# Attention front of a four-layer network: 50-row score stacks, and softmax totals spread over their rows through DRAM

## What is computed

```python
h = NUM_HEADS                       # 16, so d_k = 16
q = _proj_heads(in_features, q_proj_weight, h)
k = _proj_heads(in_features, k_proj_weight, h)
v = _proj_heads(in_features, v_proj_weight, h)
scores = jnp.einsum('bhqd,bhkd->bhqk', q, k) / sqrt(d_k) + mask
attn = jax.nn.softmax(scores, axis=-1)
out = jnp.einsum('bhqk,bhkd->bhqd', attn, v)
```

## Time and profile before

| | |
|---|---|
| median of 3 runs | 1889.87 us (1889.86 to 1893.87) |
| profiled execution, its own time | 1896.14 us |
| its span | 1894.4 us |
| granted TensorE clock, mean | 0.931 |
| PE busy | 1632.2 us, 86% |
| ACT busy | 961.6 us, 51% |
| DVE busy | 936.2 us, 49% |
| POOL busy | 489.3 us, 26% |
| SP-issued DMAs | 103.51 MB, 23.4% of 16 engines' span |

### The profile page before, as it was taken

One profiled execution on the slowest core, in us unless ns is written; L12 is line 12 of the kernel. 1 busy time (PEld: TensorE's weight loads), 2 busy tenths in 40 slices (PEclk: granted clock), 3 DMA queues, 4 the chain that ended last, 5 costly groups with the idle time before them and its releaser, 6 DMA issues. The chain is left out here.

```text
span 1894.4 us, 30936 instructions
## 1 busy us (share of the span) xinstructions
PE 1632.2 (86%) x10275; PEld 1117.4 (59%) x10276; DVE 936.2 (49%) x1793; ACT 961.6 (51%) x1531; POOL 489.3 (26%) x516
## 2 busy tenths in 40 slices
PE   5937999999999975999729999999748986898898
PEld 4822223222232224888618888888547986797787
DVE  6723434425425424777653333333275555665785
ACT  3637999999999973344332222222223334333342
POOL 3113112111111111455642222222143103000664
PEclk8968999999999986999959999999968997898999
DMA  4765056246336009321131111111122010000001
GB/s 161 197 183 80 19 79 84 33 66 85 47 50 87 17 15 309 107 83 37 68 117 48 51 52 50 53 50 50 42 95 67 23 37 20 1 1 4 23 23 45
DMA packets 75082, 125.92 MB, mean 66 GB/s; under 512 B 11169, under 2 KB 45601, under 8 KB 71841
## 3 DMA queue, kind: packets, MB, share of 16 engines
q1 hardware_dynamic: 67872, 103.51, 23.4%
q0 software_dynamic: 7104, 21.01, 3.7%
HBM read 74.63 MB, written 49.85 MB: 66 GB/s over the span
## 5 line engine op out<-in xcount | busy, mean ns | idle before, releaser
L685 ACT ACTIVATE probs<-ps_s 128x1024 f32<-128x1024 f32 (+3 forms) x640 | 513.8, 949 | 45.5 <-PE ps_s L731 42.6
L748 PE MATMUL ps_o<-probs,V 128*17 128x512 f32 (+3 forms) x2560 | 297.4, 536 | 8.5 <-POOL probs L673 8.3
L673 POOL TENSOR_SCALAR_AFFINE_SELECT probs<-probs 128x512 f32<-128x512 f32 x128 | 86.4, 677 | 459.6 <-ACT probs L685 455.7
L731 PEld LDWEIGHTS ps_s<-Q_even,K_even 64*128 64x128 f32 x640 | 56.2, 187 | 155.0 <-ACT probs L685 127.6
L731 PE MATMUL ps_s<-Q_even,K_even 64*128 64x512 f32 (+3 forms) x640 | 127.9, 448 | 22.1 <-DMA Q_even<-shift_parts 14.1
L1362 DVE COPY slot_hT<-ps_hT 128x512 f32<-128x512 f32 x72 | 49.8, 692 | 195.1 <-PE ps_hT L1405 195.1
L705 DVE RECIPROCAL inv_denominator<-ps_o 128x512 f32<-128x512 f32 x32 | 107.4, 3358 | 74.4 <-PE ps_o L762 74.4
L698 DVE COPY weighted<-ps_o 128x512 f32<-128x512 f32 x32 | 22.1, 690 | 246.9 <-PE ps_o L748 246.9
L1894 POOL TENSOR_TENSOR h_lo<-h,h_hi 128x512 fp32r<-128x512 f32 x64 | 89.5, 1415 | 185.4 <-DVE h L1940 185.4
L731 PEld LDWEIGHTS ps_s<-Q_odd,K_odd 64*128 64x128 f32 x640 | 55.2, 183 | 139.3 <-ACT probs L685 126.2
L1415 PE MATMUL ps_slot_y<-we_out,slot_hT 128*128 x576 | 136.3, 380 | 0.9 <-DVE slot_hT L1362 0.9
(11 more groups left out here) (282 smaller groups left out, 4007.4 us busy)
## 6 DMA issues: line engine op xcount, KB each, us to landing
slot_rows<-slots_in SPq DMA_DIRECT2D x72, 128.5 KB
qk_parts<-qk_hi SPq DMA_DIRECT2D x8, 1024.0 KB, 4.3
qk_parts<-qk_lo SPq DMA_DIRECT2D x8, 1024.0 KB, 7.2
Q_odd<-qk_parts SPq DMA_DIRECT2D x24, 256.0 KB
K_odd<-qk_parts SPq DMA_DIRECT2D x24, 256.0 KB
Q_even<-qk_parts SPq DMA_DIRECT2D x18, 256.0 KB
K_even<-qk_parts SPq DMA_DIRECT2D x18, 256.0 KB
X<-x SPq DMA_DIRECT2D x8, 512.0 KB, 4.4
```

The lines of the kernel that those rows point to most:

```text
L673: pool.affine_select(out=block_of, in_=block_of, compare_op=ALU.is_ge, fill=0.0, base=0, pattern=[[0, HG], [1, P]], channel_multiplier=-1) ...
L685: act.activation(probs[:, at % PROB_BUFS, 2 * p:2 * p + 2, off:BT], ps_s[:, s % SCORE_BUFS, :, off:BT], ACT.Exp).then_inc(exp_ok, 1)
L731: last = pe.matmul(ps_s[:, s % SCORE_BUFS, h, off:BT], K[j][HALF * h:HALF * h + HALF, p, t * P:(t + 1) * P], Q[j][HALF * h:HALF * h + HALF ...
L748: last = pe.matmul(ps_o[32 * h:32 * h + DH + 1, q % 2, off:BT], k["V"][:, group, SEQ_TILES * b + t, h, :], probs[:, at % PROB_BUFS, h, off ...
```

## The change

The projected q and k are stored in DRAM in the order of the stacks, each slot of a stack on its own: per block 12 DMAs of 256 KB where there were 2 of 1 MB (3 MB for 2 MB). The projection weights are permuted on chip for that (`by_head`). A unit is then loaded by 4 DMAs of 48 rows. A stack has 50 used rows in each half instead of 64, so no row is blanked; the two rows of ones come by DMA from a small table. The softmax totals no longer pass TensorE: SP stores the 17th rows of a slice to a table `totals` in DRAM (4 DMAs), waits until they landed, and loads each broadcast over its head's 16 rows (4 DMAs, `denominator`). `ps_o` is free for TensorE once VectorE has copied it.

```diff
-SHIFT_ROWS, SHIFT_PARTS = 2 * DH, 2
-SLOT_ROWS = (0, DH, 3 * DH)
+STACK_ROWS = 3 * DH
+SHIFT_PARTS = 2
+USED_ROWS = STACK_ROWS + SHIFT_PARTS
...
-STACK_LOADS = 2 * (len(Q_SLOTS) + len(K_SLOTS))
+STACK_LOADS = 4
...
-                    for n, (part, done) in enumerate(((qk_hi, hi_ok), (qk_lo, lo_ok))):
-                        sp.wait_ge(done, 4 * b + 4)
-                        to = io["qk"][n, b * BT // SEQ, :, :, :, t0:t0 + BT].rearrange("m (c g) r t -> (g r) (m c) t", c=DC)
-                        sp.dma_start(to, part[:, j].bitcast(F32)).then_inc(parts_out[j], 16)
+                    for m, slots in enumerate((Q_SLOTS, K_SLOTS)):
+                        to = io["qk"][m, b * BT // SEQ].rearrange("(c g) p s r t -> c r (g p s) t", c=DC)
+                        for wanted, part, done in ((0, qk_hi, hi_ok), (1, qk_lo, lo_ok)):
+                            for c in range(DC):
+                                sp.wait_ge(done, 4 * b + DC * m + c + 1)
+                                for row, slot in enumerate(slots):
+                                    if slot == wanted:
+                                        sp.dma_start(to[c, DH * row:DH * row + DH, :, t0:t0 + BT],
+                                                     part[:, j, DC * m + c].bitcast(F32)).then_inc(parts_out[j], 16)
...
-                pool.wait_ge(zero_ok, 1)
-                pool.wait_ge(w_lo_ok, 3)
-                blank_rows(pool, k["first_stacks"][0], k["first_stacks"][1], 1.0, blank_ok)
+                pool.memset(ones[:, :], 1.0).then_inc(ones_ok, 1)
...
 def load_stacks(eng, io, g, b, Q, K, sem):
 
-    for slots, dst, m in ((Q_SLOTS, Q, 0), (K_SLOTS, K, 1)):
-        for row, part in zip(SLOT_ROWS, slots):
-            for side in range(2):
-                src = io["qk"][part, b, m, bass.ds(g, 1)].rearrange("o (p s d) t -> s d (o p) t", s=2, d=DH)[side]
-                at = HALF * side + row
-                eng.dma_start(dst[at:at + DH].bitcast(F32), src).then_inc(sem, 16)
+    for m, stack in enumerate((Q, K)):
+        for side in range(2):
+            src = io["qk"][m, b, bass.ds(g, 1)].rearrange("o p s r t -> s r (o p) t")[side]
+            at = HALF * side
+            eng.dma_start(stack[at:at + STACK_ROWS].bitcast(F32), src).then_inc(sem, 16)
...
                     for q in range(SLICES):
+                        sp.wait_ge(sums_ok, SLICES * u + q + 2)
+                        for h in range(HG):
+                            sp.dma_start(io["totals"][q % 2, h:h + 1, :], sums[32 * h + DH:32 * h + DH + 1, q % 2]
+                                         ).then_inc(totals_out, 16)
+                        sp.wait_ge(totals_out, 16 * HG * (SLICES * u + q + 1))
+                        for h in range(HG):
+                            sp.dma_start(denominator[32 * h:32 * h + DH, q % 2],
+                                         io["totals"][q % 2, h:h + 1, :].to_broadcast([DH, BT])
+                                         ).then_inc(spread[q % 2], 16)
                         sp.wait_ge(result_ok, SLICES * u + q + 1)
...
             def _(pool):
-                blank_rows(pool, Q[1], K[1], 1.0, blank_ok)
...
                         dve.wait_ge(pv_ok, NT * u + LAST[q] + 1)
+                        if n >= 2:
+                            dve.wait_ge(spread[q % 2], 16 * HG * (n // 2))
                         dve.tensor_copy(sums[:, q % 2], ps_o[:, q % 2]).then_inc(sums_ok, 1)
...
-                        dve.wait_ge(picked_ok, n + 1)
-                        dve.reciprocal(inv[:, :], ps_o[:, q % 2]).then_inc(norm_ok, 1)
+                        dve.wait_ge(spread[q % 2], 16 * HG * (n // 2 + 1))
+                        dve.reciprocal(inv[:, :], denominator[:, q % 2]).then_inc(norm_ok, 1)
...
                     if t == 0 and n >= 2:
-                        pe.wait_ge(norm_ok, 3 * (n - 2) + 1)
+                        pe.wait_ge(sums_ok, n)
...
-                    pe.matmul(ps_o[:, q % 2], rows, sums_hi[:, :], start=True, stop=False)
-                    pe.matmul(ps_o[:, q % 2], rows, sums_lo[:, :], start=False, stop=True).then_inc(picked_ok, 1)
```

More of the change, by code:

```diff
@@ L174, in _ @@
                                base=0, pattern=[[-1, P]], channel_multiplier=1).then_inc(picked, 1)
[L176 to L180, removed]
+        @block.vector
+        def _(dve):
+            dve.wait_ge(picked, 2)
+            dve.tensor_reduce(k["head_sum"][:, :], k["ident"][:, :].rearrange("p (d h) -> p h d", d=DH), AX.X, ALU.add
+                              ).then_inc(picked, 1)
+            dve.wait_ge(picked, 3)
+            dve.tensor_copy(k["head_sel"][:, :], k["head_sum"][:, :]).then_inc(picked, 1)
 def layer_norm(k, mem, stem):
@@ L262, in phase_qkv, with raw_by_head, by_head @@
         x_view = io["x"].rearrange("(n p) d -> p n d", p=P)
+        def raw_by_head(n):
+            return w_raw[:, n].rearrange("p c (k h d) -> p (c k) h d", k=DC, d=DH)
+        def by_head(w, n):
+            order = "p c (k d h) -> p (c k) h d" if n < 2 else "p c (k h d) -> p (c k) h d"
+            return w[:, n].rearrange(order, k=DC, d=DH)
         with nc.Block() as block:
@@ L328, in _ @@
                 act.wait_ge(w_in[0], 16)
-                act.activation(w_hi[:, 0], w_raw[:, 0], ACT.Copy).then_inc(w_hi_ok, 1)
+                act.activation(by_head(w_hi, 0), raw_by_head(0), ACT.Copy).then_inc(w_hi_ok, 1)
                 highs(0, 0)
@@ L570, in _ @@
                     with pe.Fori(0, UNITS) as u:
-                        hold(pe, k, loaded, 16 * STACK_LOADS * (u + 1))
-                        for h in range(HG):
-                            side, pair = HALF * (h % 2), h // 2
-                            for t in range(QT):
-                                pe.wait_ge(masked_ok, EACH * u + QT * h + t + 1)
-                                for c in range(0, SEQ, BT):
-                                    last = pe.matmul(ps_s[:, c:c + BT], Q[side:side + HALF, pair, t * P:(t + 1) * P],
-                                                     K[side:side + HALF, pair, c:c + BT], start=True, stop=True)
-                                last.then_inc(scores_ok, 1)
+                        for pair in range(2):
+                            with pe.Fori(0, QT) as t:
+                                hold(pe, k, loaded, 16 * STACK_LOADS * (u + 1))
+                                hold(pe, k, stage_ok, 4 * QT * u + 2 * QT * pair + 2 * t + 2)
+                                for side in range(2):
+                                    hold(pe, k, masked_ok, EACH * u + 2 * QT * pair + 2 * t + side + 1)
+                                    at = HALF * side
+                                    for c in range(0, SEQ, BT):
+                                        last = pe.matmul(ps_s[:, c:c + BT], stage[at:at + STACK_ROWS, :],
+                                                         K[at:at + STACK_ROWS, pair, c:c + BT], start=True, stop=True)
+                                    last.then_inc(scores_ok, 1)
                         hold(pe, k, top_ok, EACH * u + EACH + 1)
```

118 lines of the change are left out of this document (56 added, 62 removed).

## The result

The changed kernel is slower: 1946.76 us median (1943.58 to 1951.48, 4 runs), against 1891.87 us of the kernel before (1889.86 to 1895.47, 4 runs) beside it. The ratio is 1.029, with an interval of 1.0262 to 1.0318. So it is +55 us, where +20 was forecast. The profiled execution has a span of 1944.8 us, against 1894.4.

The account below looks back on a forecast made before the run. ScalarE's exponentials were taken to set attention's pace, with TensorE close behind. Front -15, start -8, products -6, chain stalls +44 and last slice +5 summed to +20 us, so the median goes from 1889.9 to 1910 (range 1866 to 1972).

Parts of the forecast that it names:

- Front, -15 us: phase_qkv: without blanking, blocks end 9.7 us earlier, DMA sets the end, attention begins at 122 instead of 136.5 us.
- Start of attention, -8: TensorE's first weighing no longer waits 8.26 us for GpSimd's mask, which stood behind 14 us of blanking.
- The place of the stall, its victim and what stands behind it: Attention, units 2 to 6: slice 3's weighing waits some 10 us for VectorE's copy of `ps_o`; scores and ScalarE wait behind.
- Totals wait behind the loads: SP's queue at a unit's end: slice 0's totals land 17.4 us after SP is free, not 2.7: +14.7.
- the rival in which they pass the loads: Rival for SP's queue: totals are not held up, no stall, -25 us, time 1865; chance 0.06.
- One us of loading is worth 6 us in attention: Sensitivity to a unit's load time: each us more or less is 6 us in attention, 1 in front, 7 together.
- TensorE's products, -6: Attention: 64 spread products and 64 VectorE splits go, saving 0.75 to 1.2 us a unit over 8 units (0 to -10).
- Last slice, +5: End of attention: the last slice ends 13.6 us after its copy instead of 8.5.
- A slice's chain, 15.3 us: Totals' way through DRAM: stores before 3.9, totals 2.7, broadcasts 3.4, reciprocal to split 5.3 us; four slices 61.2.
- Between them I go linearly by rows: 48-row loads, rate interpolated between 125 GB/s for 16 rows and 381 for 128: 198 GB/s, 16 us a unit.
- slow loads (25 us, 1973): Rival: a unit's loads are no faster than now, 25 us, +63 over the sum, time 1973; chance 0.17.
- The rival of late small transfers: Rival: one-row stores and broadcasts cost 1.4 us more per slice, chain 81 us a unit, +33, time 1943; chance 0.13.

## Why the prediction was off

The direction and the mechanism held; one term was mis-sized, and it carries nearly the whole miss.

**Right.** *Front, -15 us*: -15.1, but by two errors that cancel. The first unit's load took some 21 us (68.5 to 90) rather than the 16 put in. Behind it the stores ran at 402 GB/s (90 to 105 us), above the quick bound of 381, and attention began less than 3 us after the last piece of DMA (before 119 us), where 2 + 5 had been put. *Start of attention, -8*: -8.0. The place of the stall, its victim and what stands behind it: `ps_o` of slice 3, once in a unit; only its length was off, 14 us of TensorE against "some 10". *Totals wait behind the loads*: 22.9 us; the rival in which they pass the loads is out. *One us of loading is worth 6 us in attention*: with 64 rows instead of 128 it takes 10 us longer from the load's issue to the next broadcasts (22.9 against 12.9), and the kernel 57.

**Roughly right.** *TensorE's products, -6*: the unit without loads is 1.5 us shorter than with the products, near -12 in all, beyond the bound of -10. *Last slice, +5*: from its copy at 752.98 to 764.04 it takes 11.1 us, not 13.6, so +2.6; the terms of the chain without the stores of the slice before (2.7 + 3.4 + 5.3 = 11.4) would have given that. *A slice's chain, 15.3 us*: 14.4.

**The step that failed** is "Between them I go linearly by rows: 125 + (48 - 16)/(128 - 16) x 256 = 198 GB/s, 16 us". Measured are 148 GB/s and 21.3 us, and then the shift rows' tail of some 3 us, which the sum had passed over; slice 0 takes 38.6 to 39 us, against 15.3 + 14.7 = 30.0. With the other slices at 14.4, the unit is 82.3 us where 75.9 stood. Units 2 to 6 were to lose 8.5 to 9 us each over 67.6 and lose 14.7, and unit 1, which was to lose 1, loses as much as they do: 88 us in place of +44. Less what the products and the last slice gave beyond their terms, that is the 37 us by which attention missed (+72.3, against -8 - 6 + 44 + 5 = +35). Of the rivals, slow loads (25 us, 1973) was nearest in kind; it was given 0.17. The rival of late small transfers, at 1943, is nearest in number, but its reason is out: a slice's chain is shorter than was summed, not longer.

A rate does not go linearly with rows. It goes by which rows they are: 16 rows 121 to 125 GB/s, 48 rows 148, or 179 when cut otherwise, 64 rows 213, 128 rows 429. 48 and 64 rows take nearly the same time, and 128 rows about half of it. The Trainium skill (SBUF — State Buffer, section "Door 1: The DMA port swizzle") gives the mapping: bits 2 to 4 of the partition's number choose one of eight clusters, bit 6 one of its two ports, so rows 32 apart share a port.
**Open.** Whether ports are the reason, and which rows are under way together; and what the 10 to 17 us in the run with a second queue consist of.

## What to carry to other kernels

Before small transfers are put into a queue, look at what stands ahead of them there once in a while: the mean share of the DMA engines (0.35 here) says nothing about a chain that meets 3 MB of loads once per unit. Sum the chain over a whole period, the held-up link included, and compare it with the engine that sets the pace; if it does not fit, cut the bulk transfer into pieces and issue each at the moment when the chain is busy on another engine. The rate of a load is not interpolated between traces with other numbers of rows: measure it with the rows that it will have, and in the cut that it will have.

## What was not expected of the hardware

- Loads by 48-row DMAs of 8 KB pieces take no less time than by 64-row ones: 21.3 us for 3.15 MB, 19.7 us for 4.19 MB; 128-row ones move 4.19 MB at 429 GB/s. The 48 rows in three other DMAs take 17.6 us.
- Behind a load, with little but its two 2-row DMAs left, DMA runs at 21 GB/s for about 3 us (234.0 to 237.5).
- Small transfers in a queue of their own still take 10.4 to 16.9 us beside a load in another, and for 8.2 us none of their pieces moves at all.
- TensorE's clock follows the stall. Windows of the changed kernel around one of them:

```profile
380.00:398.00 18.00, 17.50 (x132) 5.26 (x124) 0.00 (x0) 17.25 (x23) 2.54 (x4) 1.00 1.02 145
398.00:412.00 14.00, 0.33 (x2) 0.01 (x2) 5.60 (x5) 2.52 (x3) 0.00 (x0) 0.54 0.17 30
412.00:416.00 4.00, 3.78 (x16) 0.81 (x20) 0.17 (x1) 1.04 (x2) 0.00 (x0) 0.50 0.28 66
416.00:420.00 4.00, 4.00 (x32) 0.86 (x24) 0.00 (x0) 3.58 (x4) 0.00 (x0) 0.96 0.19 34
```

TensorE stands idle from 398 to 412, the granted clock falls to 0.50, which is 1.2 GHz, and it stays there for the first 4 us of work (eight weighings of 512 columns take 1.91 us there, 1.05 once it is back at 2.4 GHz). TensorE thus loses some 2 us more than the stall's length, an estimate from these windows. The kernel does not pay them here: VectorE's copies in these units do not wait for TensorE.
